# Shared down product of a mixture-attention kernel: from two turned hidden buffers per tile to one of 1408 columns

## The chip, the core and the metric

The kernel runs on one core of one Trainium2 chip. The metric is device time in microseconds (us) for one execution, as the median of three runs; the profile is one further execution on the same chip, whose own time is given beside its span.

## What is computed

The input x has 4 x 1024 = 4096 rows (tokens) of 512 numbers. Every row is layer-normed to xn. An attention branch gives s, a feed-forward branch with experts gives g, and the output is x + s * silu(...) of the latter:

```python
x = L0_attn_x
xn = _layernorm(x, axis=-1)
s = _L0_attn_ref(xn, qkv, o_proj, gamma, beta)
g = _silu(_L0_ffn_ref(xn, router_w, wg, wu, wd, sg, su, sd))
x = x + s * g
```

In the feed-forward branch each token goes to 2 of 8 routed experts, and in addition every token goes through one shared expert. The change concerns the shared expert alone:

```python
shared = _silu(xf @ sg) * (xf @ su) @ sd      # sg, su: 512 x 704; sd: 704 x 512
```

## The kernel before

**Two-part numbers.** A float32 operand of a product is kept as two float16 parts, high and low (value = high + low). A product of two such operands is three matmuls: high x high, high x low, low x high.

**Stages.** The program has four pieces: the weights of the attention are folded (to about 38 us), then the shared expert runs over all 32 tiles of 128 tokens while the rows are normalised and the routed experts' weights are loaded and split (to about 418 us), then 71 slot tiles of the routed experts, then the attention with the final combination.

**The shared stage.** It is a loop over s = 0 to 31, called step s here; step s handles one tile. The 704 hidden columns are two units of H = 352 (b = 0, 1; n = 2s + b numbers a unit). For each unit:

- TensorE (PE) makes the gate and up products (`unit_in`, `gate_up` at line 669: 4 chunks x 3 part pairs x 2 banks = 24 matmuls).
- ScalarE (ACT) takes `silu` (line 1350), VectorE (DVE) multiplies (`hidden`, line 1450), ACT writes the high part of the hidden values h (`h_high`, line 1356), DVE the low part (`h_low`, line 1455). They go into `h_parts[b]`, a buffer of 2 x 384 columns (352 used in each half, the rest zero from the pads that GpSimd sets once).
- SyncE (SP) issues one DMA transpose (`turn_h(n)`, line 1064) from `h_parts[b]` into `ht[b]`: 6 blocks of 128 columns.
- PE makes the down product of the unit (`unit_down`, `down` at line 676): 3 chunks x 3 part pairs = 9 matmuls of 512 columns, in one PSUM bank with the other unit's 9. ACT copies the bank out (`y_copy`, line 1370) and SP stores it.

**What sets the order.** Every engine has its own program, written out by hand, and waits on semaphores in that order. There are two buffers for h and two for the turned h, one per unit. In step s, PE runs: unit 0 in, unit 0 down of tile s-1, unit 1 in, unit 1 down of tile s-1. ACT runs: silu of unit 0, a piece of routed weights (`in_high`), `h_high` of unit 0, the high part of a normalised tile (`x_high`, line 265), `down_high`, silu of unit 1, a second `x_high` or `in_high`, `h_high` of unit 1, `y_copy`. DVE runs: statistics (`stats`), `hidden` and `h_low` of unit 0, then `normalise` (lines 253 to 261) for the tiles of that step, `down_low`, `hidden` and `h_low` of unit 1. GpSimd (POOL) makes the low part of the normalised tile (`x_low`, line 279). SP runs in step s: the turn of the normalised tiles (`turn_x`, line 284, 8 blocks), their store (line 290) and the next load of x (line 1023), then `turn_h(2s-1)`, loads of routed weights, the store of y, and `turn_h(2s)`.

**Single and double steps.** Six tiles (5, 9, 13, 17, 21, 25) are normalised early but put off to the end of the shared stage, so that six steps (s = 3, 6, 9, 12, 15, 18) normalise two tiles; these are called double steps, the other steps from 0 to 23 single steps. Steps 24 to 31 normalise nothing.

**Semaphores around the change.** `h_turned[b]` tells that a turn of unit b has landed. `unit_down` waits for it, and so does `h_high` of the same unit one tile later, since it writes into the buffer that the turn reads:

```python
def h_high(n, b):
    act.wait_ge(h_ready, n + 1)
    wait(act, h_turned[b], n // 2 * 16)
    nc.scalar.copy(h_parts[b][:, 0, 0:H], sbuf[b]).then_inc(h_hi, 1)
```

`turn_h(n)` waits for `h_lo` (its low part is written) and for `y_done` (the unit's former down product has read `ht[b]`).

**End of the stage.** In steps 27 to 30, DVE makes one-hot tables for the routing (`one_hot`, lines 926 and 928) and PE multiplies them (`hot_product`, line 1270), in pairs right behind the down product of unit 0.

## Time and profile before

| | us |
|---|---|
| median of three runs | 1183.19 (1182.62 to 1183.99) |
| the profiled execution's own time | 1181.17 |
| its span, first to last instruction | 1179.4 |
| PE busy | 1141.0 (97%), 6598 matmuls |
| DVE, ACT, POOL busy | 575.2 (49%), 471.7 (40%), 419.3 (36%) |
| gate and up products, line 669, x3240 | 506.1 |
| down products, line 676, x1215 (576 of them of the shared expert) | 286.0 |

PE is busy nearly all the time, but matmuls overlap one another in this profile: the durations of line 676 have a mean of 381 ns, while a row of nine starts every 1.88 us. What a matmul costs is read from when the next one starts. From 38 to 325 us the DMA engines are busy 0.89 of the time. The wait column of a line says how long its engine was idle just before, and who ended that.

### The profile page before, as it was taken

What the parts mean: (1) busy time and instruction counts of PE and PEld (TensorE: products, weight loads), DVE (VectorE), ACT (ScalarE), POOL (GpSimd) and SP (SyncE); (2) the same over time, 40 slices, a digit from 0 to 9 for tenths busy, and PEclk for the clock granted to TensorE, in tenths of its full rate; (3) what the DMA queues carried; (4) which work ended last, traced back from release to release, by engine and by line L of the source; (5) the groups of instructions that cost most, each with busy time, mean ns of one, the idle gap of its engine ahead of it and who ended that gap; (6) DMA issues with size and microseconds to landing.
All of it is one profiled execution on the core that took longest, in us unless ns stands there. A gap on an engine that the chain in (4) does not pass through costs nothing. (4 is left out here: it accounts for less than half of the span.)

```text
span 1179.4 us, 21120 instructions
## 1 busy us (share of the span) xinstructions
PE 1141.0 (97%) x6598; PEld 627.2 (53%) x6599; DVE 575.2 (49%) x1168; ACT 471.7 (40%) x824; POOL 419.3 (36%) x659
## 2 busy tenths in 40 slices
PE   8699999999999999999999999999999999999995
PEld 4355555555555555555555555554444444444442
DVE  6676776676558421212212212212476476476476
ACT  5444434444322222322322322324654544645642
POOL 2253333332100122222222222213754754753753
PEclk9999999999999999999999999999999999999998
DMA  9979899899533588898987777876774766865363
GB/s 291 244 181 220 216 230 209 200 212 234 156 88 74 120 174 204 201 202 204 206 196 188 183 179 174 182 154 157 161 180 141 170 172 168 170 157 159 119 156 98
DMA packets 370594, 210.22 MB, mean 178 GB/s; under 512 B 308816, under 2 KB 322136, under 8 KB 370272
## 3 DMA queue, kind: packets, MB, share of 16 engines
q1 hardware_dynamic: 359696, 173.68, 64.0%
q0 software_dynamic: 10800, 35.69, 11.4%
q8 instruction: 36, 0.59, 0.2%
q14 instruction: 30, 0.25, 0.1%
q10 hardware_dynamic: 32, 0.02, 0.0%
HBM read 89.31 MB, written 46.01 MB: 115 GB/s over the span
## 5 line engine op out<-in xcount | busy, mean ns | idle before, releaser
L669 PE MATMUL pair<-arena 128*128 (+2 forms) x3240 | 506.1, 313 | 1.7 <-DMA arena<-arena 1.7
L669 PEld LDWEIGHTS pair<-arena 128*128 128x128 f16 x3240 | 316.2, 98 | 184.5 <-issue 2.7
L676 PE MATMUL bank<-arena 128*128 (+1 forms) x1215 | 286.0, 381 | 10.2 <-DMA arena<-arena 10.2
L676 PEld LDWEIGHTS bank<-arena 128*128 128x128 f16 x1215 | 118.9, 98 | 138.1 <-issue 11.8
L1515 DVE SCALAR_TENSOR_TENSOR arena<-pair,slot_unit,arena 128x352 f32<-128x352 f32 x71 | 41.4, 584 | 269.3 <-ACT arena L1431 201.7
L1431 ACT ACTIVATE arena<-pair,slot_unit 128x352 f32<-128x352 f32 x71 | 39.3, 553 | 205.7 <-PE pair L669 181.8
L1194 POOL COPY arena<-token_of 128x1 uint32 (+1 forms) x71 | 13.0, 183 | 279.8 <-issue 124.9
L1794 PE MATMUL bank<-arena 128*128 128x512 f16 x432 | 98.6, 379 | 6.7 <-DMA arena<-arena 6.7
L1781 PE MATMUL pair<-arena 128*128 128x512 f16 (+3 forms) x576 | 98.9, 326 | 2.5 <-ACT arena L1839 2.5
L1196 POOL DMA_INDIRECT arena<-xn_rows,arena x71 | 70.8, 998 | 55.6 <-POOL arena L1194 51.7
L1766 PE MATMUL bank<-arena 128*128 128x512 f16 x384 | 86.0, 379 | 1.6 <-PEq L1018 1.6
L1766 PE MATMUL pair<-arena 128*128 128x512 f16 x384 | 84.7, 379 | 0.0
L1781 PEld LDWEIGHTS pair<-arena 128*128 128x128 f16 x576 | 52.7, 98 | 49.3 <-ACT arena L1839 4.5
L1701 POOL DMA_INDIRECT arena<-slot_rows,arena x64 | 68.0, 1062 | 24.2 <-POOL arena L1698 22.4
L1350 ACT ACTIVATE arena<-pair,unit 128x352 f32<-128x352 f32 x64 | 35.1, 549 | 103.1 <-PE pair L669 101.5
L235 POOL TENSOR_TENSOR root_seed<-variances,minus_half 128x2 f32<-128x2 f32 x32 | 25.0, 781 | 132.6 <-DVE variances L245 132.6
L1794 PEld LDWEIGHTS bank<-arena 128*128 128x128 f16 x432 | 41.2, 98 | 56.3 <-DMA arena<-arena 10.2
L1708 POOL TENSOR_TENSOR arena<-arena 128x512 f32<-128x512 f32 x32 | 40.6, 1267 | 75.3 <-ACT arena L1853 75.0
L1766 PEld LDWEIGHTS bank<-arena 128*128 128x128 f16 x384 | 37.5, 98 | 46.2 <-issue 2.0
L1766 PEld LDWEIGHTS pair<-arena 128*128 128x128 f16 x384 | 37.6, 98 | 45.3
L1450 DVE SCALAR_TENSOR_TENSOR arena<-pair,unit,arena 128x352 f32<-128x352 f32 x64 | 37.0, 578 | 48.4 <-ACT arena L1350 48.2
L1719 POOL TENSOR_TENSOR arena<-arena 128x512 f32<-128x512 f32 x32 | 41.2, 1288 | 50.6 <-DVE arena L1945 50.3
(184 smaller groups left out, 1183.5 us busy)
## 6 DMA issues: line engine op xcount, KB each, us to landing
slot_rows<-arena SPq DMA_DIRECT2D x71, 256.0 KB
arena<-in_L_attn_x_dram SPq DMA_DIRECT2D x64, 256.0 KB, 3.5
xn_rows<-arena SPq DMA_DIRECT2D x32, 260.0 KB, 2.5
shared_rows<-arena SPq DMA_DIRECT2D x32, 256.0 KB
arena<-shared_rows SPq DMA_DIRECT2D x32, 256.0 KB
out_dram<-arena SPq DMA_DIRECT2D x32, 256.0 KB, 2.4
arena<-in_L_ffn_wg_dram SPq DMA_DIRECT2D x32, 176.0 KB, 3.0
arena<-in_L_ffn_wu_dram SPq DMA_DIRECT2D x32, 176.0 KB, 3.2
```

The source lines that it names most:

```text
L669: last = pe.matmul(bank[:, 0:width], xt[:, a, c, :], weights(c, b, col, width), start=(c == 0 and i == 0), stop=(c == KC - 1 and i == 2))
L676: last = pe.matmul(bank[:, :], ht[:, a, c, :], weights(c, b), start=(start and c == 0 and i == 0), stop=(stop and c == HC - 1 and i == 2))
L1196: pool.indirect_dma_start(xg[u].bitcast(U32), None, xn_rows.bitcast(U32), bass.IndirectOffsetOnAxis(ap=index[u], axis=0)).then_inc(gathere ...
L1431: nc.scalar.activation(sbuf[u], g_banks[u][:, 0:H], ACT.Silu, scale=slot_unit[u][:, 0:1]).then_inc(slot_silu_done, 1)
L1450: v.scalar_tensor_tensor(sbuf[b], u_banks[b][:, 0:H], unit[:, t, 1:2], sbuf[b], ALU.mult, ALU.mult).then_inc(h_ready, 1)
L1515: v.scalar_tensor_tensor(sbuf[u], u_banks[u][:, 0:H], slot_unit[u][:, 1:2], sbuf[u], ALU.mult, ALU.mult).then_inc(slot_h_ready, 1)
L1701: pool.indirect_dma_start(c[f"y{n}", u], None, slot_rows, bass.IndirectOffsetOnAxis(ap=c[f"i{n}", u], axis=0)).then_inc(y_loaded[n][u], 16)
L1708: pool.tensor_tensor(c["y0", u], c["y0", u], c["y1", u], ALU.add).then_inc(y_summed, 1)
L1719: pool.tensor_tensor(c["res", u], c["s", u], c["x", t % X_AHEAD], ALU.add).then_inc(res_ready, 1)
L1766: last = pe.matmul(bank[:, :], left, right, start=(k == 0 and n == 0), stop=(k == KC - 1 and n == 2))
L1781: last = pe.matmul(wide[t % 2][:, col:col + w], qt[:, a, k, i * P:(i + 1) * P], x2t[b % 2][col // HALF][:, r, k, 0:w], start=(k == 0 and m ...
L1794: last = pe.matmul(pv_banks[t % 2][:, :], c["pt", t % 2][:, a * (i + 1) + k, :], vs[:, k, r, :], start=(k == 0 and n == 0), stop=(k == i a ...
```

## The change

Both units' rows of h go into one buffer `h_row` of 11 x 128 = 1408 columns: 704 high values, then 704 low values. 704 is five and a half blocks of 128, so the sixth block holds the last 64 high and the first-written 64 low values side by side. One DMA transpose a tile turns all 11 blocks into one buffer `h_row_turned`. The weights sd are laid out to match (`shared_down[part, chunk]`): in the sixth chunk the high part holds the last 64 rows twice, the low part holds them once and zeros below. A tile's down product is then 5 x 3 + 2 = 17 matmuls and stands behind unit 1's gate and up products. `h_low` of unit 1 becomes two instructions (288 and 64 columns). The pads of `h_parts` are written at the start of the slot stage, by ACT. The buffers `h_row` and `h_row_turned` have no second copy.

```diff
-        shared_down, end = carve(end, [NS, HC, 2, D], F16)
+        shared_down, end = carve(end, [2, MAIN + 1, D], F16)
...
-                    def turn_h(n):
-                        b = n % 2
-                        sp.wait_ge(h_lo, n + 1)
-                        wait(sp, y_done, n - 1)
-                        sp.dma_start_transpose(ht[b].rearrange("p s c t -> p (s c) t"),
-                                               h_parts[b].rearrange("p s n -> p (s n)")).then_inc(h_turned[b], 16)
+                    def turn_h(t):
+                        sp.wait_ge(h_lo, 2 * t + 2)
+                        wait(sp, y_done, t)
+                        sp.dma_start_transpose(h_row_turned, h_row).then_inc(h_turned, 16)
...
                         if s > 0:
-                            turn_h(2 * s - 1)
+                            turn_h(s - 1)
...
-                        turn_h(2 * s)
...
-                    def unit_down(n, b):
-                        t = n // 2
-                        pe.wait_ge(h_turned[b], (t + 1) * 16)
-                        if b == 0:
-                            wait(pe, y_ready, t - 1)
-                        down(pe, ht[b], lambda c, s: shared_down[:, b, c, s, :], y_bank[t % 2],
-                             b == 0, b == 1).then_inc(y_done, 1)
+                    def tile_down(t):
+                        pe.wait_ge(h_turned, (t + 1) * 16)
+                        wait(pe, y_ready, t - 1)
+                        bank = y_bank[t % 2]
+                        for c in range(MAIN):
+                            for left, part in ((c, 0), (c, 1), (MAIN + 1 + c, 0)):
+                                pe.matmul(bank[:, :], h_row_turned[:, left, :], shared_down[:, part, c, :],
+                                          start=(c == 0 and left == 0 and part == 0), stop=False)
+                        for part in range(2):
+
+                            last = pe.matmul(bank[:, :], h_row_turned[:, MAIN, :], shared_down[:, part, MAIN, :],
+                                             start=False, stop=(part == 1))
+                        last.then_inc(y_done, 1)
...
-                            if s > 0:
+                            if s > 0 and b == 1:
                                 if s == 1:
-                                    pe.wait_ge(shared_lo, IN_SPLITS + 2 * (b + 1))
-                                unit_down(n - 2, b)
+                                    pe.wait_ge(shared_lo, len(splits))
+                                tile_down(s - 1)
...
                     def h_high(n, b):
                         act.wait_ge(h_ready, n + 1)
-                        wait(act, h_turned[b], n // 2 * 16)
-                        nc.scalar.copy(h_parts[b][:, 0, 0:H], sbuf[b]).then_inc(h_hi, 1)
+                        wait(act, h_turned, n // 2 * 16)
+                        nc.scalar.copy(h_row[:, b * H:(b + 1) * H], sbuf[b]).then_inc(h_hi, 1)
...
                         dve.wait_ge(h_hi, n + 1)
-                        v.tensor_tensor(h_parts[b][:, 1, 0:H], sbuf[b], h_parts[b][:, 0, 0:H], ALU.subtract
-                                        ).then_inc(h_lo, 1)
+                        cols, low = slice(b * H, min((b + 1) * H, MAIN * P)), (MAIN + 1) * P
+                        count = cols.stop - cols.start
+                        main = v.tensor_tensor(h_row[:, low + cols.start:low + cols.stop], sbuf[b][:, 0:count],
+                                               h_row[:, cols], ALU.subtract)
+                        if b == 0:
+                            main.then_inc(h_lo, 1)
+                        else:
+                            tail = MAIN * P
+                            v.tensor_tensor(h_row[:, tail + TAIL:tail + 2 * TAIL], sbuf[b][:, count:H],
+                                            h_row[:, tail:tail + TAIL], ALU.subtract).then_inc(h_lo, 1)
```

PE before, from the last matmul of unit 0 in step 3 to the first of step 4 (L669 gate and up, L676 down; a row is a matmul or a run of them):

```order
L669 MATMUL pair<-arena 128x352
L676 MATMUL bank<-arena 128x512 [waits y_ready,h_turned0]
L676 MATMUL bank<-arena 128x512 x8
L669 MATMUL pair<-arena 128x352 [waits h_ready,x_turned0]
L669 MATMUL pair<-arena 128x352 x23
L676 MATMUL bank<-arena 128x512 [waits h_turned1]
L676 MATMUL bank<-arena 128x512 x8
L669 MATMUL pair<-arena 128x360 [waits logits_kept,h_ready,x_turned1]
```

PE in the changed kernel, the same place (L679 gate and up, L1259 and L1263 down):

```order
L679 MATMUL pair<-arena 128x352
L679 MATMUL pair<-arena 128x352 [waits h_ready,x_turned0]
L679 MATMUL pair<-arena 128x352 x23
L1259 MATMUL bank<-arena 128x512 [waits y_ready,h_turned]
L1259 MATMUL bank<-arena 128x512 x14
L1263 MATMUL bank<-arena 128x512 x2
L679 MATMUL pair<-arena 128x360 [waits logits_kept,h_ready,x_turned1]
```

The nine matmuls between the two units have moved behind unit 1, less one, and PE waits for a turn once a step.

SP before, step 3 (L284 turn of a normalised tile, L290 its store, L1023 load of x, L1064 turn of h, L1053 load of routed weights, L1058 store of y):

```order
L284 DMA_TRANSPOSE arena<-arena 128x8x128 [waits x16_lo,gu_done]
L290 DMA xn_rows<-arena 128x520 [waits x16_lo]
L1023 DMA arena<-in_L_attn_x_dram 128x512 [waits x16_lo]
L1064 DMA_TRANSPOSE arena<-arena 128x6x128 [waits y_done,h_lo]
L1053 DMA arena<-in_L_ffn_wd_dram 128x512 [waits down_lo]
L1058 DMA shared_rows<-arena 128x512 [waits y_ready]
L1064 DMA_TRANSPOSE arena<-arena 128x6x128 [waits y_done,h_lo]
```

SP in the changed kernel, the same step (L293, L299, L1033, L1073, L1063, L1068 in the same roles):

```order
L293 DMA_TRANSPOSE arena<-arena 128x8x128 [waits x16_lo,gu_done]
L299 DMA xn_rows<-arena 128x520 [waits x16_lo]
L1033 DMA arena<-in_L_attn_x_dram 128x512 [waits x16_lo]
L1073 DMA_TRANSPOSE arena<-arena 128x11x128 [waits y_done,h_lo]
L1063 DMA arena<-in_L_ffn_wd_dram 128x512 [waits down_lo]
L1068 DMA shared_rows<-arena 128x512 [waits y_ready]
```

The turn of unit 0 at the end of the step is gone; the remaining turn has 11 blocks in place of 6 and still stands behind the turn of the normalised tile, its store and the load of x.

ACT before, from `h_high` of unit 0 in a single step to that of unit 1 (L1356 `h_high`, L265 `x_high`, L1364 `down_high`, L1350 silu, L1360 `in_high`):

```order
L1356 CAST arena<-arena 128x352 [waits h_turned0,h_ready]
L265 CAST arena<-arena 128x512 [waits x_turned0,xn_stored1,xn_ready]
L1364 ACTIVATE arena<-arena 128x512 [waits down_loaded]
L1350 ACTIVATE arena<-pair,unit 128x352 [waits h_lo,gu_done]
L1360 ACTIVATE arena<-arena 128x704 [waits in_loaded1]
L1356 CAST arena<-arena 128x352 [waits h_turned1,h_ready]
```

ACT in the changed kernel, the same place:

```order
L1365 CAST arena<-arena 128x352 [waits h_turned,h_ready]
L274 CAST arena<-arena 128x512 [waits x_turned0,xn_stored1,xn_ready]
L1373 ACTIVATE arena<-arena 128x512 [waits down_loaded]
L1359 ACTIVATE arena<-pair,unit 128x352 [waits h_lo,gu_done]
L1369 ACTIVATE arena<-arena 128x704 [waits in_loaded1]
L1365 CAST arena<-arena 128x352 [waits h_turned,h_ready]
```

The order is the same; `h_high` of unit 0 now waits for the one turn of the tile before, not for the earlier turn of unit 0 alone.

## Rows read from the trace of the kernel before

**Rows 1.** Stages: us, busy us of each engine (instructions), granted PE clock, DMA share, GB/s.
```profile
38.00:325.00 287.00, 277.48 (x1704) 161.63 (x1705) 190.06 (x466) 119.74 (x215) 96.56 (x190) 0.99 0.89 209
325.00:418.00 93.00, 92.04 (x600) 54.65 (x599) 53.96 (x143) 23.79 (x43) 6.80 (x13) 1.00 0.44 95
```

**Rows 2.** Timeline, weight loads of one step: start us, us, engine, line, operation.
```profile
149.94 1.76 PEld L676 LDWEIGHTS bank<-arena 128*128 128x128 f16 x9
...
151.82 3.60 PEld L669 LDWEIGHTS pair<-arena 128*128 128x128 f16 x24
...
155.46 1.76 PEld L676 LDWEIGHTS bank<-arena 128*128 128x128 f16 x9
...
161.03 1.76 PEld L676 LDWEIGHTS bank<-arena 128*128 128x128 f16 x9
```

**Rows 3.** Timeline, single step 10: from unit 0's high part to the turn.
```profile
164.31 0.48 ACT L1356 CAST arena<-arena 128x352 f16<-128x352 f32 x1 [1.70 <-DVE arena L1450]
...
165.12 0.52 DVE L1455 TENSOR_TENSOR arena<-arena 128x352 f16<-128x352 f32 x1
...
166.34 0.55 DVE L261 TENSOR_SCALAR arena<-arena,mean_var,kept 128x512 f32<-128x512 f32 x1
...
167.94 1.16 POOL L279 TENSOR_TENSOR arena<-arena 128x512 f16<-128x512 f32 x1
...
169.17 1.31 SPq L284 DMA_TRANSPOSE arena<-arena  x1
...
171.68 1.22 SPq L1064 DMA_TRANSPOSE arena<-arena  x1
```

**Rows 4.** Timeline, double step 9: the same path with two tiles.
```profile
151.49 0.48 ACT L1356 CAST arena<-arena 128x352 f16<-128x352 f32 x1 [0.65 <-DVE arena L1450]
...
152.72 0.52 DVE L1455 TENSOR_TENSOR arena<-arena 128x352 f16<-128x352 f32 x1
...
155.18 0.55 DVE L261 TENSOR_SCALAR arena<-arena,mean_var,kept 128x512 f32<-128x512 f32 x1
...
159.55 1.24 SPq L284 DMA_TRANSPOSE arena<-arena  x1
...
161.99 1.42 SPq L1064 DMA_TRANSPOSE arena<-arena  x1
```

**Rows 5.** Line view of L1064, single issues at 282.0, 128.4 and 82.6 us.
```profile
DMA to landing us min/median/max: 3.1/3.1/3.1
...
DMA to landing us min/median/max: 4.4/4.4/4.4
...
DMA to landing us min/median/max: 5.0/5.0/5.0
```

**Rows 6.** Line view over the whole run: L1064 (6 blocks), then L284 (8 blocks).
```profile
DMA to landing us min/median/max: 2.7/3.2/10.8
...
DMA to landing us min/median/max: 3.0/3.2/11.5
```

**Rows 7.** Timeline, steps 1 to 3 of the shared stage.
```profile
57.31 4.00 PE L676 MATMUL bank<-arena 128*128 128x512 f16 x9 [7.69 <-DMA arena<-arena]
...
59.40 1.22 SPq L1064 DMA_TRANSPOSE arena<-arena  x1
...
68.21 6.92 POOL L1160 MEMSET arena<- 32x8192 f16 x1
...
82.64 1.22 SPq L1064 DMA_TRANSPOSE arena<-arena  x1
...
87.72 2.12 PE L676 MATMUL bank<-arena 128*128 128x512 f16 x9 [0.63 <-DMA arena<-arena]
```

**Rows 8.** Timeline, start of step 25, and a one-hot product in step 28.
```profile
325.03 3.78 PE L669 MATMUL pair<-arena 128*128 128x360 f16 x24
...
364.94 0.45 PE L1270 MATMUL bank<-arena 128*128 128x71 f16 x8 [0.55 <-DVE arena L928]
```

**Rows 9.** Stages, columns as in Rows 1: just behind PE's longest wait.
```profile
58.00:61.00 3.00, 3.00 (x8) 1.03 (x7) 2.02 (x4) 2.67 (x5) 0.00 (x0) 0.50 0.78 245
```

More of the change, by code:

```diff
@@ L149, in mixture_attention_kernel @@
         sbuf, end = carve_ring(end, 2, [H], F32)
+        TAIL = NS * H % P
+        MAIN = NS * H // P
+        HOLD = 2 * MAIN + 1
+        assert 2 * TAIL == P
+        h_row, _ = carve(end, [HOLD * P], F16)
         h_parts, end = carve_ring(end, 2, [2, HP], F16)
+        h_row_turned, _ = carve(end, [HOLD, P], F16)
         ht, end = carve_ring(end, 2, [2, HC, P], F16)
+        assert HOLD <= 4 * HC
         y_out, end = carve(end, [D], F32)
@@ L220, in split_hi @@
             act.wait_ge(loaded, count)
-            nc.scalar.activation(target(0), src, ACT.Copy, scale=S_W).then_inc(shared_hi, 1)
+            nc.scalar.activation(target(0), src(0), ACT.Copy, scale=S_W).then_inc(shared_hi, 1)
         def split_lo(dve, n):
@@ L403, in sync @@
                     load_in(n)
-                for b in range(NS):
-                    rows, whole = sd[b * H:(b + 1) * H, :], (HC - 1) * P
-                    sp.dma_start(raw_down[:, b, 0:HC - 1, :], rows[0:whole, :].rearrange("(c p) n -> p c n", p=P)
-                                 ).then_inc(shared_down_loaded[b], 16)
-                    sp.dma_start(raw_down[0:HR, b, HC - 1, :], rows[whole:H, :]).then_inc(shared_down_loaded[b], 16)
+                sp.dma_start(raw_down[:, 0:2, :], sd[0:2 * P, :].rearrange("(c p) n -> p c n", p=P)
+                             ).then_inc(shared_down_loaded[0], 16)
+                sp.dma_start(raw_down[:, 2:MAIN, :], sd[2 * P:MAIN * P, :].rearrange("(c p) n -> p c n", p=P)
+                             ).then_inc(shared_down_loaded[1], 16)
+                for r in range(2):
+                    sp.dma_start(raw_down[r * TAIL:(r + 1) * TAIL, MAIN, :], sd[MAIN * P:, :]
+                                 ).then_inc(shared_down_loaded[1], 16)
                 for t in range(2):
@@ L1149, in _ @@
                     fold_gpsimd(pool)
-                    for u in range(2):
-                        pool.memset(h_parts[u][:, :, H:HP], 0.0).then_inc(pads, 1)
-                        pool.wait_ge(pads, u + 1)
                     seed(pool, 2, 0)
@@ L1407, in slot_h_high @@
                         if early(j, 2):
-                            act.wait_ge(h_turned[u], NT * 16)
+                            act.wait_ge(h_turned, NT * 16)
+                            act.wait_ge(consts, CONSTS)
+                            nc.scalar.activation(h_parts[u][:, :, H:HP], zero_source, ACT.Copy, scale=0.0).then_inc(pads, 1)
                         else:
```

40 lines of the change are left out of this document (21 added, 19 removed).

## The prediction

> **What bounds the kernel now.** I read the busy time by stage first. From 38 to 325 us PE is busy 277.5 of 287.0 us, while DVE, ACT and POOL are busy 190, 120 and 97 us [rows 1]: PE is the bound of the shared stage, and the others look idle. The weight loads give its pace: nine matmuls of a down product every 1.88 us (149.94 to 151.82), 24 of a gate-and-up product every 3.64 us (to 155.46), and a step of 11.09 us from one unit 0's down product to the next (149.94 to 161.03) [rows 2]. One matmul of 512 columns thus costs 1.88 / 9 = 0.21 us.
>
> Then I followed what must arrive before each down product, and there the reading turns. The chain in a single step [rows 3] begins when ACT writes unit 0's high part (164.31). DVE writes the low part (165.12) and, next in its program, normalises a coming tile (its last instruction at 166.34); ACT and POOL make that tile's parts (POOL starts at 167.94 and takes 1.16), SP turns it (169.17), stores it, loads the next x, and only then turns h (171.68). In a double step two tiles are normalised and turned in between: 151.49 to 161.99 [rows 4]. Before the change this chain is open: `h_high` of unit 0 waits for the turn of unit 0, which SP issued at the end of the former step, ahead of the normalised tile. So PE sets the pace.
>
> **The change part by part.**
>
> *Removed: one matmul in 18 per tile.* 32 x 0.21 = 6.7 us, all on PE's path, which is the whole gain on offer.
>
> *Moved: the down product, behind unit 1.* PE now needs the turn of a step 1.88 us earlier than it needed unit 1's turn, since unit 0's nine matmuls no longer stand in front. From the start of a step that is 2 x 3.64 = 7.28 us.
>
> *Changed: one turn of 11 blocks for two of 6.* SP saves one issue of 1.22 us a step, off the path. The remaining turn is wider. The shortest landing is 2.7 us at 6 blocks and 3.0 at 8 [rows 6], or 0.15 us a block; five more blocks cost 0.75 us. Behind a turned tile, a store and a load, turns of 6 blocks landed between 3.1 and 4.4 us after their issue [rows 5]; I take the middle, 3.75, and 4.5 us for 11 blocks. The bounds are no extra cost (3.75) and a cost in proportion to the width from the shortest landing (2.7 x 11 / 6 = 4.95, so 2.25 more, 6.0). I take the slope between the two widths because both are transposes of the same queue.
>
> The Trainium skill (page "SBUF — State Buffer", section "The DMA setup-cost knee") says that a transfer costs a fixed 2 us or so plus its bytes at 436 GB/s, and asks for fewer, larger transfers. By it five more blocks (164 KB) would cost an estimated 0.38 us in place of 0.75, and the sum below would be 21 x 0.37 = 8 us lower. The rows give twice that slope, so the sum goes by the rows.
>
> *Added: a wait that closes a loop.* With one `h_row`, `h_high` of unit 0 in step s waits until the turn of tile s-1 has landed. That turn stands on SP behind the tile normalised in step s-1, and the tile of step s stands on DVE behind `h_low` of unit 0. So from landing to landing the program now runs: `h_high`, `h_low`, normalise, `x_high`, `x_low`, turn of the tile, store, load, turn of h, landing. Nothing on PE lies in it. Its length:
>
> - Single step: 171.68 - 164.31 = 7.37 us [rows 3], less 0.3 that `h_low` stood behind another DVE instruction (164.79 to 165.12; with a late `h_high` that is done), plus 0.05 for the wake-up, plus 4.5 for the landing: 11.6 us.
> - Double step: 161.99 - 151.49 = 10.50 us [rows 4], less 0.7 for the same reason (151.97 to 152.72), plus 0.05 and 4.5: 14.35 us.
>
> PE's own step is 11.09 - 0.21 = 10.88 us. The loop is longer by 0.7 us in a single and 3.5 us in a double step. What is queued behind the waiting `h_high` on ACT (`x_high`, `down_high`, unit 1's silu) is either in the loop itself or has the 8 us from there to the next landing. The second instruction of unit 1's `h_low` (64 columns, about 0.2 us) ends at about the time at which SP comes to the turn, and I charge nothing.
>
> *When it starts to bind.* At the start PE stands from 49.6 to 57.3 us for DMA [rows 7]. Now unit 1's gate and up come first there. They reuse the banks that `hidden` of the tile before frees, and that ended about 1.1 us before SP's issue at 59.40, for the high and low parts of 0.48 and 0.52 us [rows 3] lie between: at 58.3, an estimated 1.0 us after 57.31. The turn then lands in time behind them. The microsecond is left out, being small beside what follows. PE restarts at half clock (0.50 from 58 to 61) [rows 9] with either product. In step 2 POOL's 6.92 us memset at 68.21 holds the next tile back, and the turn of step 3 goes out at 82.64 and lands 5.0 us later [rows 5, 7]; PE already waited 0.63 us for it, from 87.1. With 0.75 added it lands at 88.4, and PE, which now asks 1.88 us earlier, waits. From there the loop sets the pace up to the turn of tile 23: 21 links, of them 6 double (steps 3 to 18) and 15 single (to step 23): 15 x 11.6 + 6 x 14.35 = 260.1 us. The last turn lands at 348.5, and 17 x 0.21 = 3.6 us later, at 352.1, step 25 can begin. It began at 325.03 [rows 8]. **The loop costs 27.0 us** by then, the 25 saved matmuls included.
>
> *After it.* Steps 24 and on normalise nothing, so the loop falls open and PE leads. The remaining eight tiles save 8 x 0.21 = 1.7 us. Against that, the pairs of one-hot products stand behind unit 0's gate and up alone, and come 1.88 us earlier against DVE's tables; PE already waited 0.55 us for one [rows 8]. If DVE catches up after the first of three pairs this costs 1.9 us, if it never does 5.6; I take 3.6. The last turn may hold PE for 0.3 us, left out. The two small pad instructions on ACT run beside PE's next product and cost nothing. The slot stage and attention are as before.
>
> **Sum.** 27.0 - 1.7 + 3.6 = +28.9 us on the profiled execution of 1181.17 gives 1210.1; the median of the runs shown lies 2.0 above it, so I forecast **1212 us**, 2.4% slower.
>
> **Rivals.**
>
> *The stalls come one by one (loop not closed).* If `h_high` is never held long enough to shift the tile behind it, only the places with little slack pay: the turns of steps 3, 4 and 5, and those behind the five later double steps. Each pays 1.88 + 0.75 less its slack; in step 3 the slack is nothing (PE waited [rows 7]), in the double steps a few tenths: about 2.2 us each, 9 places, 20 us. With the 6.7 us of saved matmuls and the 3.6 us of the one-hot tables: 20 - 6.7 + 3.6 = +17, or 1200 us. For it: ACT is busy only 120 of 287 us. Against: program order counts here, not busy share, and rows 3 show each link directly behind the other.
>
> *Everything stays hidden; faster.* The mechanism: with unit 0's turn gone, SP and the DMA queue are free earlier, the turn of a step goes out 2 us sooner and lands within 7.28 us of the step's start. It decides at a landing below 2.8 us: a single link is then 7.1 + 2.8 = 9.9, 1.0 under PE's step, and the two single steps between double ones make up the 1.8 us by which a double link (9.85 + 2.8) is too long. Time: 1183.2 - 6.7 = 1176.5 us. For it: the shortest landing of 6 blocks is 2.7. Against: at 8 blocks no row shows less than 3.0 [rows 6].
>
> *The landing grows with the width in proportion.* 6.0 in place of 4.5 us in 21 links: +31 more, 1243 us. Against: 6 to 8 blocks grew by 0.3, not by 0.9.
>
> *PE at half clock after each wait.* The rows show it once, after 7.69 us of idle; the waits forecast here are 0.7 and 3.5 us. PE's slack in a loop-bound step absorbs part of it, so I give it no time of its own, and up to 5 us in the range.
>
> **How the numbers follow.** Loop as worked out: 0.71. Its own range is 1200 to 1224, from 0.5 us more or less per link (10.5 us) and the one-hot bounds. One by one: 0.15. In proportion: 0.05. Everything hidden: 0.05. Gain and losses equal: 0.04. The range for 8 in 10 reaches from 1195 (below the second case) to 1228. About 0.2% (2.4 us) is what a measurement of this kernel can tell from no change: faster 0.05, within it 0.04, slower 0.91.
>
> **What would show it.** In the changed profile: 17 down matmuls a tile, 544 in all; landings of the wide turn near 4.5 us; ACT's `h_high` of unit 0 waiting for a DMA in nearly every step up to 23; steps of 11 to 12 us and of 14 to 15 us after the double ones, with PE waiting for "DMA arena" at the down product, some 25 us in total; step 25 beginning near 352 us; PE busy share down, other stages unchanged. I am wrong if step 25 begins before 335 us, if `h_high` waits for DVE as now, or if the wide turn lands in under 3.5 us.

## The result, and the profile after

The changed kernel takes 1221.67 us (median of four runs, 1220.03 to 1223.97) against 1183.59 us of the kernel before on the same chip (four runs, 1182.62 to 1184.73). The ratio is 1.0316, with a 95% interval of 1.0297 to 1.0334: 38 us slower. 1212 us was forecast, with a range of 1195 to 1228. The profiled execution took 1220.03 us (span 1218.3), so 38.9 us more span than before.

The shared stage in the changed kernel (columns as in [rows 1]; first the stretch of the first of those rows, then the stretch that the changed program needs for about the same work):

```profile
38.00:325.00 287.00, 255.94 (x1518) 145.64 (x1519) 181.40 (x455) 106.92 (x195) 89.48 (x175) 0.94 0.76 189
...
38.00:352.00 314.00, 282.45 (x1673) 160.72 (x1674) 197.17 (x491) 117.90 (x215) 96.14 (x190) 0.95 0.75 188
```

In the same 287 us PE is busy 255.9 us in place of 277.5 and starts 186 matmuls fewer. DVE, ACT, POOL and the DMA engines are all less busy too, so no engine has become the bound. What PE and ACT wait for (engine, line waited for, us in total, times, longest us):

```profile
PE bank L1259 <- DMA arena<-arena: 25.2, 10, 4.4
PE bank L1815 <- DMA arena<-arena: 12.3, 9, 2.0
PE pair L679 <- DVE arena L1463: 7.8, 1, 7.8
...
PE bank L1278 <- DVE arena L938: 3.5, 3, 2.5
```
```profile
ACT arena L1365 <- DMA arena<-arena: 76.4, 24, 6.7
```

PE's 25.2 us at the down product (L1259) are close to the forecast "some 25 us"; 23.1 of them lie in the loop, and 2.1 at the last turn, far behind it. The 7.8 us at L679 are the start, where the prediction expected this wait for `hidden`. ACT's row is the wait that the prediction named as the cause: `h_high` waits 24 times for a DMA, the turn of the tile before. The kernel before has no such wait in its list. Step 25 begins here, where it began at 325.03 before [rows 8]:

```profile
349.91 3.40 PE L1259 MATMUL bank<-arena 128*128 128x512 f16 x15
353.15 0.59 PE L1263 MATMUL bank<-arena 128*128 128x512 f16 x2
353.58 7.36 PE L679 MATMUL pair<-arena 128*128 128x360 f16 x48
```

So the 38.9 us of span are 28.6 up to step 25 (353.58 - 325.03), 4.9 from there to the slot stage (its third silu: 421.15 before, 454.64 now, 33.5 later), nothing in the slot stage, and 5.4 in the attention stage (373.9 us before, 379.2 now), whose code is the same. These figures compare one profiled execution of each kernel.

One single link of the loop in the changed kernel (the path of [rows 3], timeline of step 22, from unit 0's high part to the next one):

```profile
327.54 0.48 ACT L1365 CAST arena<-arena 128x352 f16<-128x352 f32 x1 [2.33 <-DMA arena<-arena]
...
328.05 0.53 DVE L1470 TENSOR_TENSOR arena<-arena 128x352 f16<-128x352 f32 x1 [1.93 <-ACT arena L1365]
329.28 0.55 DVE L270 TENSOR_SCALAR arena<-arena,mean_var,kept 128x512 f32<-128x512 f32 x1
...
330.88 1.16 POOL L288 TENSOR_TENSOR arena<-arena 128x512 f16<-128x512 f32 x1
332.12 1.25 SPq L293 DMA_TRANSPOSE arena<-arena  x1
...
334.42 1.40 SPq L1073 DMA_TRANSPOSE arena<-arena  x1
...
339.06 0.48 ACT L1365 CAST arena<-arena 128x352 f16<-128x352 f32 x1 [2.83 <-DMA arena<-arena]
```

Up to the turn of h, every row starts within 1.1 us of the end of the one above it: 6.88 us from the high part to the turn of h (L1073), 4.64 to its landing, 11.5 us in all. A double link (the path of [rows 4], step 3):

```profile
87.40 0.48 ACT L1365 CAST arena<-arena 128x352 f16<-128x352 f32 x1 [3.50 <-DMA arena<-arena]
...
92.03 1.25 SPq L293 DMA_TRANSPOSE arena<-arena  x1
...
94.77 1.24 SPq L293 DMA_TRANSPOSE arena<-arena  x1
...
97.21 1.68 SPq L1073 DMA_TRANSPOSE arena<-arena  x1
...
101.98 1.46 PE L1259 MATMUL bank<-arena 128*128 128x512 f16 x3 [3.57 <-DMA arena<-arena]
102.01 0.48 ACT L1365 CAST arena<-arena 128x352 f16<-128x352 f32 x1 [5.86 <-DMA arena<-arena]
```

9.81 us to the turn, 4.80 to the landing, and PE and ACT are released within 0.03 us of each other.

### The profile page after: what moved, and what is told of

Same layout as the page of the kernel before. It is cut to its first block and busy times, and to the rows that moved or that the text cites. A ratio compares the mean times of both kernels' runs of the same rounds, so it can differ in the third digit from the quotient of the medians.

```text
span 1218.3 us, 21023 instructions
## 1 busy us (share of the span) xinstructions
PE 1147.4 (94%) x6566; PEld 626.2 (51%) x6567; DVE 582.4 (48%) x1200; ACT 470.4 (39%) x826; POOL 415.9 (34%) x657
## 3 DMA queue, kind: packets, MB, share of 16 engines
q0 software_dynamic: 10800, 35.69, 11.5%
## 5 line engine op out<-in xcount | busy, mean ns | idle before, releaser
L679 PE MATMUL pair<-arena 128*128 (+2 forms) x3240 | 505.6, 314 | 9.9 <-DVE arena L1463 7.8
L679 PEld LDWEIGHTS pair<-arena 128*128 128x128 f16 x3240 | 317.4, 98 | 191.5 <-issue 10.7
L686 PE MATMUL bank<-arena 128*128 x639 | 149.3, 379 | 1.3 <-DMA arena<-arena 1.3
L1259 PE MATMUL bank<-arena 128*128 128x512 f16 x480 | 118.8, 404 | 25.2 <-DMA arena<-arena 25.2
L1815 PE MATMUL bank<-arena 128*128 128x512 f16 x432 | 98.6, 379 | 12.3 <-DMA arena<-arena 12.3
L686 PEld LDWEIGHTS bank<-arena 128*128 128x128 f16 x639 | 62.5, 98 | 67.7 <-issue 1.8
L1259 PEld LDWEIGHTS bank<-arena 128*128 128x128 f16 x480 | 48.3, 103 | 88.2 <-DMA arena<-arena 29.7
L1787 PE MATMUL bank<-arena 128*128 128x512 f16 x384 | 86.0, 379 | 1.6 <-PEq L1028 1.6
L1802 PEld LDWEIGHTS pair<-arena 128*128 128x128 f16 x576 | 52.7, 98 | 49.0 <-ACT arena L1860 4.2
L1365 ACT CAST arena<-arena 128x352 f16<-128x352 f32 x64 | 31.0, 485 | 114.1 <-DMA arena<-arena 76.4
L1815 PEld LDWEIGHTS bank<-arena 128*128 128x128 f16 x432 | 41.2, 98 | 61.9 <-DMA arena<-arena 15.8
L1729 POOL TENSOR_TENSOR arena<-arena 128x512 f32<-128x512 f32 x32 | 40.6, 1268 | 78.7 <-ACT arena L1874 78.6
L1787 PEld LDWEIGHTS bank<-arena 128*128 128x128 f16 x384 | 37.5, 98 | 46.3 <-issue 2.1
```

What stands on the lines that cost most here:

```text
L679: last = pe.matmul(bank[:, 0:width], xt[:, a, c, :], weights(c, b, col, width), start=(c == 0 and i == 0), stop=(c == KC - 1 and i == 2))
L686: last = pe.matmul(bank[:, :], ht[:, a, c, :], weights(c, b), start=(start and c == 0 and i == 0), stop=(stop and c == HC - 1 and i == 2))
L1259: pe.matmul(bank[:, :], h_row_turned[:, left, :], shared_down[:, part, c, :], start=(c == 0 and left == 0 and part == 0), stop=False)
L1729: pool.tensor_tensor(c["y0", u], c["y0", u], c["y1", u], ALU.add).then_inc(y_summed, 1)
L1787: last = pe.matmul(bank[:, :], left, right, start=(k == 0 and n == 0), stop=(k == KC - 1 and n == 2))
L1802: last = pe.matmul(wide[t % 2][:, col:col + w], qt[:, a, k, i * P:(i + 1) * P], x2t[b % 2][col // HALF][:, r, k, 0:w], start=(k == 0 and m ...
```

## The experiments

Twelve kernels, in four groups. "Step 25" is the time at which its first matmul starts in the profiled execution: 325.0 us before, 353.6 in the changed kernel. Where no number of runs is given, a kernel ran once. Nineteen runs of the kernel before spread over 5 us, so single totals that differ by less say nothing, and the readings rest on the rows. Of each edit the lines that decide are shown. The kernel before took 1186.14 us on the chip of the first four, 1181.1 (median) beside e8 to e11, 1183.25 beside e12 and e13, 1181.99 beside e14 and e15.

### Is it the move of the down product, or the one buffer?

**e6**: the kernel before, with both down products (18 matmuls, two turns, two buffers each) behind unit 1.

```diff
-                            if s > 0:
+                            if s > 0 and b == 1:
...
-                                unit_down(n - 2, b)
+                                unit_down(2 * s - 2, 0)
+                                unit_down(2 * s - 1, 1)
```

> The kernel before with one thing of the change: both units' down products of a tile stand behind unit 1's gate and up on PE (18 matmuls, two buffers, two turns of 6 blocks as before). Loop theory: no loop, only the eight turns that had little slack pay for the 1.88 us, about 12 us in all, step 25 begins near 337 us. One-by-one theory: this is most of the change's loss, step 25 begins near 345 us or later.

Measured: 1188.54 us, 2.4 more than before, which one run of each can't tell from no change. Step 25 begins 3.3 us late (328.33; 337 was expected), and the turns are late by little (PE's waits at the down products, L676):

```profile
PE bank L676 <- DMA arena<-arena: 5.0, 7, 1.3
```

Six of the seven waits stand behind double steps, 0.45 to 0.73 us each; the longest is in the slot stage, as before the change. So the move alone does not cost 28 us: with narrow turns and two buffers, late by a little costs a little. What is left for the buffer and the wide turn is the greater part. e1 shows next what the move costs with the wide turn.

**e1**: the changed kernel with a second `h_row` (`h_high` waits for the turn of two tiles before). To make room, expert 7's down rows share expert 6's place, and its tokens are computed with those.

```diff
-                        wait(act, h_turned, n // 2 * 16)
-                        nc.scalar.copy(h_row[:, b * H:(b + 1) * H], sbuf[b]).then_inc(h_hi, 1)
+                        wait(act, h_turned, (n // 2 - 1) * 16)
+                        nc.scalar.copy(h_rows[n // 2 % 2][:, b * H:(b + 1) * H], sbuf[b]).then_inc(h_hi, 1)
```

> The changed kernel with a second h row, so that the high part of a tile waits for the turn two tiles back and not for the last one (to make room, the routed weights of expert 7 are stored over those of expert 6 and its tokens use expert 6). Loop theory: the loop through the normalised tile is open, ACT hardly waits for a DMA before unit 0's high part, and only the double steps still hold PE, since their wide turn lands 4.4 + 4.5 = 8.9 us into a step that asks at 7.3: 6 x 1.7 us, about 3 us at the start, a little in single steps. Step 25 begins near 336 us instead of 353.5. One-by-one theory (the down product asks earlier for a wider turn, no loop): nothing that it names has changed, step 25 begins at 353 as in the changed kernel.

Measured: 1214.05 us, step 25 at 346.59, where the loop theory expected 336. `h_high` no longer waits for a DMA, and single steps run at PE's own pace (10.87 us), as that theory has it. But only 7 of the 28.6 us come back: the double steps still make PE wait, 2.3 to 3.3 us each in place of the 1.7 expected, and five of these six waits are followed by a slower product, which the expectation left out (timeline of PE; the number in brackets is the idle time before):

```profile
PE bank L1261 <- DMA arena<-arena: 17.9, 7, 3.3
```
```profile
139.30 5.10 PE L1261 MATMUL bank<-arena 128*128 128x512 f16 x15 [2.48 <-DMA arena<-arena]
...
152.16 3.40 PE L1261 MATMUL bank<-arena 128*128 128x512 f16 x15
```

15 matmuls take 5.10 us after the wait and 3.40 in the next step. So a second buffer opens the loop, and behind it a second path shows that is nearly as long: SP's order, in which two normalised tiles stand ahead of the wide turn of h. The loop sets the pace of the changed kernel, but opening it alone leaves step 25 21.6 us later than before.

### Opening the loop by order alone

**e3**: DVE normalises the coming tiles ahead of unit 0's low part, and ACT makes `x_high` ahead of unit 0's high part. Both leave the loop, and one buffer stays (the diff shows DVE's half).

```diff
+                        for t in normal_in(s):
+                            normalise(dve, t)
                         h_low(2 * s, 0)
...
-                        for t in normal_in(s):
-                            normalise(dve, t)
```

> The changed kernel with normalise ahead of unit 0's low part on DVE and the tile's high part ahead of unit 0's high part on ACT; SP's order and the one h row as changed. Loop theory: the tile no longer hangs on the landing of the last turn, the loop is open, step 25 begins near 336 us as with two rows. One-by-one theory: the turn of h still stands behind the same tile on SP, step 25 begins near 353 us.

Measured: 1205.06 us, step 25 at 341.32 (336 expected), 12.3 us earlier than in the changed kernel. `h_high` waits 7 times for a DMA, 7.2 us in all, in place of 24 times and 76.4 us; single steps are 10.87 us. Again the double steps are left:

```profile
PE bank L1259 <- DMA arena<-arena: 15.4, 7, 3.3
```

**e2**: on SP, the turn of h ahead of the turn of the normalised tiles in every step.

```diff
+                        if s > 0:
+                            turn_h(s - 1)
                         for t in routed_in(s):
                             if t > 1:
                                 turn_x(t)
...
-                        if s > 0:
-                            turn_h(s - 1)
```

> The changed kernel with SP's turn of h put ahead of the turn of the normalised tile in each step, one h row as changed. Loop theory: the normalised tile drops out of the loop, what is left (high part, normalise, unit 1's hidden and low part, turn, landing: 7.2 + 4 us) is about 11.2 us against PE's 10.9, so step 25 begins near 330 us. One-by-one theory: the turn goes out 2.5 to 4.4 us sooner in every step, all its waits go, step 25 begins near 322 us.

Measured: 1247.34 us, step 25 at 386.0. Neither theory has this. PE's waits:

```profile
PE pair L679 <- DVE arena L1463: 35.9, 13, 9.3
PE bank L1259 <- DMA arena<-arena: 19.2, 14, 2.0
```

L1463 is `hidden`, for which the next gate-and-up product needs its banks free. The load of the next x now stands on SP behind the turn of h, which waits for `h_low`; the statistics of that x stand at the head of DVE's program, ahead of `hidden` and `h_low`. They wait 76.5 us for loads of x (16.8 in the kernel before). This is a new loop through SP's and DVE's order, as read from the rows; no run takes it apart. In step 7 of this kernel the turn of h goes out at 144.71, the load behind it at 148.35, and the load's landing starts the statistics 3.6 us later:

```profile
144.71 1.40 SPq L1073 DMA_TRANSPOSE arena<-arena  x1
...
148.35 0.43 SPq L1033 DMA_DIRECT2D arena<-in_L_attn_x_dram  x1
...
151.94 0.69 DVE L250 BATCH_NORM_STATS2 moments<-arena 128x6 f32<-128x512 f32 x1 [7.26 <-DMA arena<-in_L_attn_x_dram]
...
153.15 0.58 DVE L1463 SCALAR_TENSOR_TENSOR arena<-pair,unit,arena 128x352 f32<-128x352 f32 x1
...
153.76 0.49 ACT L1365 CAST arena<-arena 128x352 f16<-128x352 f32 x1 [9.05 <-DVE arena L1463]
```

**e11**: the changed kernel, with SP turning h in double steps between the two tiles instead of behind both.

```diff
                             if t + 2 < NT:
                                 load_x(t + 2)
+                            if len(routed_in(s)) == 2 and t == routed_in(s)[0]:
+                                turn_h(s - 1)
...
-                        if s > 0:
+                        if s > 0 and len(routed_in(s)) < 2:
                             turn_h(s - 1)
```

> The changed kernel with only SP's order in double steps altered: turn of h of the tile before right behind the first tile, ahead of the second. Loop theory: the loop stays closed, so single links stay at 11.6 us; in the 6 double links the second tile's part of the chain (x_high, x_low, turn, store, load, some 2.5 us) falls out, so they shrink from 14.75 to about 12.3 us: step 25 begins 6 x 2.5 = 15 us earlier, near 339 us, total about 1207. Rival (the waits come one by one and not from a loop): the single steps too go back to PE's 10.9 us and step 25 begins below 330 us. Rival (the next tile, turned later, holds the next step up as much as it saved): step 25 stays at 350 or later.

Measured: 1198.13 us (1207 expected), step 25 at 336.42 (339 expected). The loop is still closed, as `h_high` waiting for the DMA shows (86.15 to 97.75 us is the double step 3, with the turn of h between the two tiles):

```profile
86.15 0.48 ACT L1367 CAST arena<-arena 128x352 f16<-128x352 f32 x1 [2.99 <-DMA arena<-arena]
...
90.77 1.24 SPq L293 DMA_TRANSPOSE arena<-arena  x1
...
93.87 1.64 SPq L1073 DMA_TRANSPOSE arena<-arena  x1
95.64 1.50 SPq L293 DMA_TRANSPOSE arena<-arena  x1
...
97.75 0.48 ACT L1367 CAST arena<-arena 128x352 f16<-128x352 f32 x1 [2.85 <-DMA arena<-arena]
```

From step 3 to step 24 the 21 links take 246.3 us (86.15 to 332.43). 15 x 11.6 + 6 x 12.3 = 247.8 was expected. The single links are 11.66 us on average, the double ones 11.91. This is the sharpest test of the loop: one edge was shortened, the single links stayed as they were, and the sum fell by 15.9 us (from 262.2 in the changed kernel), where the shorter links give 14.4. The rest by which the total beat its expectation lies behind step 25.

**e8**: the diffs of e3 and e11 together.

> The reordering of e3 (DVE normalises the coming tiles ahead of unit 0's low part, ACT makes x_high of them ahead of unit 0's high part), and in double steps SP turns h of the tile before right behind the first of the two tiles, ahead of the second. Loop theory (what is left in e3 is the second tile that stands ahead of the turn of h on SP in double steps; e3 had 15.4 us of such waits in 7 places and half clock after them): with the second tile out of the way the turn goes out about 2.5 us earlier, the waits fall to a few us in all, steps are 10.9 us, step 25 begins at 320 to 325 us and the profile reads about 1183 to 1188. Rival (the wide transfer itself is too long for the 7.3 us between the step's start and the down product, whatever stands ahead of it): the waits of the double steps stay at 2 us each, step 25 stays near 341 us, 1203 to 1206. Second rival (as in e2, loads of x that now stand behind the turn arrive late and hold the statistics at the head of DVE's program): PE's waits move to hidden (bank free) and the total stays above 1200.

Measured: 1185.01 us, step 25 at 322.44, 31 us earlier than in the changed kernel and 2.6 earlier than before. PE's waits for the turn and the clock of the stretch (columns as in [rows 1]):

```profile
PE bank L1261 <- DMA arena<-arena: 4.3, 4, 2.2
```
```profile
38.00:325.00 287.00, 277.81 (x1697) 161.84 (x1698) 191.59 (x491) 117.79 (x216) 101.29 (x190) 0.98 0.82 207
```

Both rivals fall: with one tile instead of two ahead of it, the wide transfer nearly fits in the 7.3 us (in the shared stage one wait of 1.5 us and two below 0.4; the 2.2 us are the last turn), and the statistics wait 10.6 us for loads of x, less than before (16.8). 277.8 us busy is what the kernel before had (277.5). The total is still 3.9 us above the kernel before.

### What comes behind the loop

**e9**: e8, with the one-hot products of unit 0 moved behind unit 1's gate and up, ahead of the down product.

```diff
+                                for m in hot_products_in(s, 0):
+                                    hot_product(m)
                                 tile_down(s - 1)
...
-                            for m in hot_products_in(s, b):
+                            for m in hot_products_in(s, b) if b == 1 else ():
```

> e8 with the one-hot products that stood behind unit 0's gate and up moved behind unit 1's, ahead of the down product, in steps 26 to 31. Theory (the products came 1.88 us earlier than before against DVE's tables; the changed kernel waited 3.5 us for the tables): that wait falls to under 1 us and the time is 2 to 3 us under e8. Rival (DVE's tables are the bound in these steps, so that the wait only moves to the next product): no change against e8.

Measured over ten runs: 1185.19 us, ratio to before 1.0027 (1.0015 to 1.0038). The wait for DVE's tables is gone from the list. From the end of tile 24's product to that of tile 29 it is 56.8 us (337.11 to 393.90), in e8 60.8 (333.47 to 394.24): 4 us. They do not show in the total, though 2 to 3 us were expected: step 25 began 3.6 us later in this execution (326.08), and two turns came late behind it, tile 30's (1.9 us) and the last (2.5 us).

**e10**: e9, with the last down product behind the gate and up of both first slot tiles.

```diff
                         slot_in(j, j, 0)
-                        if j == 0:
-                            tile_down(NT - 1)
+                    tile_down(NT - 1)
```

> e9 with the down product of the last tile behind both first slot tiles' gate and up instead of behind the first. Theory (the last turn came 2.1 us late in the changed kernel and the 17 matmuls after that wait ran at half clock, 1.7 us more): both go, 3 to 4 us under e9, and with all of PE's waits in the loop gone the 32 saved matmuls (6.7 us) show: 1177 to 1181 us, below the kernel before. Rival (the last turn is late anyway, or the second slot tile waits for a buffer behind it): the same as e9, within 1 us.

Measured over ten runs: 1183.54 us (1177.93 to 1190.99), ratio 1.0015 (0.9993 to 1.0038). The last product no longer waits. The gain over e9, 1.65 us, is half of what was expected, and tile 30's product still waits:

```profile
403.50 3.41 PE L1261 MATMUL bank<-arena 128*128 128x512 f16 x15 [2.02 <-DMA arena<-arena]
...
414.34 3.40 PE L1261 MATMUL bank<-arena 128*128 128x512 f16 x15
```

**e15**: the changed kernel with its loop left closed, and only the diffs of e9, e10 and e12 (below).

> The changed kernel with the loop left as it is, and only what comes behind it altered: one-hot products behind unit 1's gate and up, last down product behind both first slot tiles' gate and up, slot turn behind the turn of h. It tells two things. First, the price of the prediction's part after the loop: step 25 stays near 353.5 us, the wait for DVE's tables (3.5 us) and the late last turn (2.1 us of wait and 1.7 of half clock) go, so the slot stage starts some 6 to 7 us earlier, at 447 to 449 us in place of 454.6 (rival: under 2 us, if DVE's tables or the last turn are late wherever they stand). Second, whether the 5.4 us by which the changed kernel's attention stage, whose code is the same, was longer than before's (379.2 against 373.8 us) belongs to it: if so, it stays at 378 to 380 here and the total is about 1214; if it is a matter of the single execution, it is 374 to 377 and the total 1208 to 1212.

Measured: 1205.77 us. Step 25 begins at 352.57, 1.0 us earlier than in the changed kernel; the slot stage (third silu) at 445.66 in place of 454.64. So what comes behind the loop was worth 8.0 us, a little above the 6 to 7 expected. The attention stage takes 373.6 us.

### Versions that beat both

**e12**: e10 with SP's first slot turn behind the turn of tile 30's h.

```diff
-                        if s == NT - 1:
-                            turn_slot_x(0)
                         if s > 0 and len(routed_in(s)) < 2:
                             turn_h(s - 1)
+                        if s == NT - 1:
+                            turn_slot_x(0)
```

> e10 with SP's first turn of a slot tile put behind the turn of tile 30's h instead of ahead of it. In e9 and e10 the turn of tile 30 went out at 399.2 and 399.6 us, behind that slot turn (398.2 in e10), and PE waited 1.9 and 2.0 us for it. Theory (SP's order alone makes it late): the wait goes and the time is about 2 us under e10, so 1181 to 1182 where the kernel before has 1181. Rival (the slot turn is now late for the first slot tile, or the turn of h is late by itself): no change against e10.

Measured over twelve runs: 1180.75 us, ratio 0.9979 (0.9967 to 0.9991). The wait for tile 30's turn is gone.

**e13**: e12 with unit 1's high and low parts ahead of the split of routed weights, on ACT and on DVE (the diff shows ACT's half).

```diff
                         silu(2 * s + 1, 1)
+                        h_high(2 * s + 1, 1)
                         for i in in_chunks(s)[1:]:
                             in_high(i)
-                        h_high(2 * s + 1, 1)
```

> e12 with unit 1's high part ahead of the split of routed weights on ACT, and its low part ahead of that split on DVE. In e10's double step at 98 to 112 us the high part started at 104.03 behind 0.79 us of that split, and the low part (104.96) behind another 0.89. Theory (the turns of the double steps go out late by these two): they go out about 1.2 us earlier there, the waits left in the shared stage (3.2 us, and half clock behind one) fall to under 1.5 us, and the time is 1 to 4 us under e12: 1177 to 1180, below the kernel before. Rival (the landing is long because of the traffic beside it, 5.9 us for that turn, so that an earlier issue only lands as late): the same as e12. Rival (the split of routed weights is now late and the routing's DMAs with it): slower than e12.

Measured over twelve runs: 1179.12 us, ratio 0.9964 (0.9950 to 0.9978): 4 us faster than the kernel before and, by the two ratios, 42 us faster than the change as given. In the profiled execution, the fastest of the twelve (1174.23 us):

```profile
PE pair L679 <- DVE arena L1464: 8.3, 1, 8.3
PE bank L1816 <- DMA arena<-arena: 6.3, 7, 1.4
...
PE bank L1261 <- DMA arena<-arena: 2.9, 4, 1.3
```
```profile
38.00:325.00 287.00, 275.63 (x1702) 161.21 (x1703) 193.06 (x491) 117.32 (x216) 99.90 (x190) 0.99 0.83 207
```

All of the waits for a turn of h come to 2.9 us, from 25.2; under 1.5 was expected. No down product behind a wait is slow any more (granted clock 0.99 in this stretch, 0.94 in the changed kernel). The first rival is partly right: the turn of tile 4 went out about 0.5 us earlier after the turn before it than in e12, not 1.2, and still took 5.8 us to land.

**e14**: the control. The kernel before, with the diffs of e3, e12 and e13.

> A control: the kernel before (two turns of 6 blocks, 18 matmuls a tile, each unit's down product in its old place) with those of e13's reorderings that it can have: normalisation and x_high ahead of unit 0's parts, unit 1's parts ahead of the split of routed weights, the slot turn behind the turn of h. Theory (in the kernel before the turns of the shared stage arrive in time, 1.2 us of waits in 62 to 330 us, so that there is nothing for the reorderings to win, and what e13 has over it comes from the 32 saved matmuls): within 0.2% of the kernel before, 1181 to 1185 where that has 1183. Rival (the reorderings make the gain by themselves): 3 to 5 us faster, as e13 is. Rival (the turn of unit 0 stands at the end of a step, and is made late by the normalisation ahead of it): slower by 2 us or more.

Measured over five runs: 1207.34 us, ratio 1.0219 (1.0199 to 1.0239), 25 us slower. The theory (no change) falls; the last rival is right, and by far more than it said (8.7 us of these waits are at the start, where before had 7.7):

```profile
PE bank L676 <- DMA arena<-arena: 28.1, 13, 8.7
```

The double step 9, first its start in the kernel before, then the same step in e14:

```profile
146.47 3.78 PE L669 MATMUL pair<-arena 128*128 128x360 f16 x24
```
```profile
156.37 3.78 PE L669 MATMUL pair<-arena 128*128 128x360 f16 x24
...
167.28 0.48 ACT L1356 CAST arena<-arena 128x352 f16<-128x352 f32 x1
...
168.35 1.22 SPq L1064 DMA_TRANSPOSE arena<-arena  x1
...
175.97 1.22 SPq L1064 DMA_TRANSPOSE arena<-arena  x1
...
179.69 3.34 PE L676 MATMUL bank<-arena 128*128 128x512 f16 x9 [2.86 <-DMA arena<-arena]
```

The high part of unit 0 starts 10.9 us after the start of the step (156.37 to 167.28) in place of 5.0 (146.47 to 151.49 [rows 4]), since it now stands behind the normalised tiles. Its turn goes out late (168.35), and so does all that stands behind it on SP: the two tiles' turns and then the turn of unit 1 (175.97, 19.6 us after the start in place of 15.5). PE's large waits are for that turn of unit 1: six of them, one behind each double step, come to 14.6 us.

So this set of reorderings brings nothing to the kernel before. The turn between two tiles (e11), and these moves without the one that puts normalisation first, were not tried on it; but it has only 1.2 us of waits for turns between 62 and 330 us and 1.0 us for DVE's tables, so that order could have won little there. What e13 has over it is near the 32 saved matmuls (6.7 us) less the waits that were added; no run takes that apart.

## Why the prediction was right, step by step

The forecast was 28.9 us over the profiled execution, and 38.9 were measured; sign and mechanism were right. Of the 10.0 us missed, 1.6 lie up to step 25, 3.0 from there to the slot stage, and 5.4 in the attention stage, where the cause is open. So most of the miss lies behind the loop.

- *The loop.* 21 links were forecast at 260.1 us and took 262.2 (87.40 to 349.59). Single links: 11.6 forecast, 11.58 on average (10.5 to 13.0). Double: 14.35 forecast, 14.75. The parts fit too: in twelve of the fifteen single links the turn goes out 7.0 us after `h_high` (7.12 forecast), and what spreads is the landing, 3.6 to 5.6 us. Step 25 was forecast at 352.1 and began at 353.6. e3 opens the loop by order and e1 by a buffer, and with either the single steps fall to PE's 10.87 us; e11 shortens one edge and moves the sum by about what it should. That the loop sets the pace is shown. It is not the only cause that suffices: with the loop open, the double steps alone still put step 25 16.3 us (e3) and 21.6 us (e1) later than before. The prediction had this second path only as a rival ("one by one"), not beside the loop, and without the slower product. (24 tiles are done by step 25, not 25; the sum does not use that number.)
- *Where it starts to bind.* Landing at 88.4 forecast, 87.4 measured, in step 3 as said.
- *The wide landing.* 4.5 us and 0.05 for the wake-up forecast, 4.54 from issue to `h_high` on average over steps 3 to 22; no row shows the wake-up by itself. Where the DMA engines are less busy (0.36 to 0.58 of the time), 3.5 us were read in e13 (the line of the turn of h, 296 to 360 us); the shortest landings of 6 and 8 blocks were 2.7 and 3.0 [rows 6]:

```profile
DMA to landing us min/median/max: 3.5/3.5/3.5
```

  That is 0.16 us a block, near the 0.15 taken, and the proportional rival (5.0 at least) falls. The Trainium skill's page "SBUF — State Buffer", section "The DMA setup-cost knee", would have given an estimated 0.08 us a block, half that slope; the measurement decides against it for these transposes.
- *PE at half clock after each wait.* It was given no time of its own. It is there behind five of the six double steps: after the wait of 4.39 us the granted clock is 0.50, the lower of the two levels, from 141 to 145 us. Behind the sixth, after a wait of 3.63 us, the product runs at full speed:

```profile
141.00:145.00 4.00, 4.00 (x10) 1.36 (x9) 2.29 (x7) 2.16 (x5) 1.77 (x5) 0.50 0.72 246
```
```profile
294.28 3.41 PE L1259 MATMUL bank<-arena 128*128 128x512 f16 x15 [3.63 <-DMA arena<-arena]
```

  In the changed kernel the time that PE has over in the next links takes it, as argued: in the three links where the turn goes out later than usual, the rows show a longer step on SP, POOL or DVE, and no wait for PE. In e1 and e3, where the loop is open, it is paid: 1.7 us (5.10 against 3.40 us for 15 matmuls) behind five double steps in e1 and three in e3.
- *After it: -1.7 + 3.6.* The net was forecast at 1.9 us; 4.9 came. The one-hot products were within their bounds (3.5 us of waits in place of 1.0). **The term that was mis-sized is "the last turn may hold PE for 0.3 us, left out":** it came 2.13 us late, and the product behind it ran at the lower clock, 1.7 us more, so -1.7 + 2.5 + 3.8 = 4.6 of the 4.9 us:

```profile
441.91 5.10 PE L1259 MATMUL bank<-arena 128*128 128x512 f16 x15 [2.13 <-DMA arena<-arena]
```

  e15, which moves the three pieces behind the loop and nothing else, wins 8.0 us there.
- *"The slot stage and attention are as before."* The slot stage is. The attention stage took 5.4 us longer, in waits for turned probabilities (12.3 us at L1815, 6.7 before). It took 378.8 us in e1 and 373 to 377 in all others, among them e15, with the same closed loop, and e11. So it does not follow from the loop. What sets it is open; no run here was made on that stage, and the forecast's "as before" missed by more here than anywhere else.
- *The rivals.* "One by one" (1200 us) counts nine places where it names eight, which would make it 1198. Its mechanism is real in an open chain: with the narrow turn it costs at most 0.7 us a place (e6), with the wide one 2.3 to 3.3 us (e1; 2.2 assumed), and mostly a slower product besides. What fails is its condition, since `h_high` is held in nearly every step. "Everything hidden" asked for a landing under 2.8 us, and no landing of 11 blocks that was read was under 3.5. Yet its time (1176.5) is nearly reached by e13 (1179.1) with another order and such landings.

## What to carry to other kernels

Before a second buffer is given up, write down what stands between the release of the buffer and its next release in program order, on every queue, DMAs too, and add it up: if that sum exceeds the pace of the bounding engine, it is the new pace, however idle the engines in it look. Then look for links that are in the loop only by the order of the code; here two moved calls and a turn put between two tiles brought back 31 us, where a second buffer alone brought 7. Opening a loop uncovers the next path, which can be nearly as long. And an order belongs to the kernel for which it was made: the moves of e3, e12 and e13 made the kernel before 25 us slower.

## What was not expected of the hardware

- A PE wait of 2 to 4 us can be followed by a stretch at the lower clock: 17 matmuls took up to 6.1 us there (140.81 to 146.90) in place of 3.7. In the kernel before, only the longest wait, at the start, showed this [rows 9]. A late turn can thus cost PE its wait and some 1.7 us more. It does not always: the length of the wait alone does not decide, for 2.13 us was followed by the slow product in the changed kernel (441.91), 3.63 us in the same kernel was not (294.28), nor was 2.02 us in e10 (403.50). What decides is not shown here.
- The wide turn's landing spreads from 3.5 to 6.6 us in e13; the turn of 103 us took 5.8 us, while from 296 to 360 us, where the DMA engines are less busy, all took 3.5. The total of e10 spread over 13 us in ten runs, where the kernel before spread over 5 in nineteen; why is not shown.
